# Cross-attention with low-rank weights: contexts computed for two groups at once, and Wo's low-rank part folded in earlier batches

## The reference

```python
def _lora_linear(x, W, A, B):
    return x @ W + SCALING * (x @ A @ B)          # R = 16, SCALING = 2
q = _lora_linear(hidden_states, Wq, Aq, Bq)       # 32 heads
k = _lora_linear(traces, Wk, Ak, Bk)              # 8 heads, each repeated for 4 query heads
v = _lora_linear(traces, Wv, Av, Bv)
scores = jnp.einsum('bhqd,bhtd->bhqt', q, k) / jnp.sqrt(HD)
attn = jax.nn.softmax(scores, axis=-1)
context = jnp.einsum('bhqt,bhtd->bhqd', attn, v)
out = _lora_linear(context, Wo, Ao, Bo)
return hidden_states + out
```

## Time and profile before

| | |
|---|---|
| timed executions | 675.72, 675.79, 678.38 us; median 675.79 |
| profiled execution | 678.06 us, its span 676.3 us |
| mean granted clock of PE | 0.947 |
| busy in the span | PE 98%, weight loads 78%, DVE 76%, ACT 69%, POOL 56% |
| contexts (L1532) | 1024 hardware matmuls, 70.3 us |
| DMA | 125.07 MB, 59.6% of 16 engines' time |

### The profile page before, as it was taken

The page is one execution under the profiler, slowest core; times in us unless marked ns, Lnnn a source line. Parts: engine busy times, 40 slices in busy tenths (PEclk is TensorE's granted clock), DMA queues, the critical chain, the costliest instruction groups (busy, mean ns, idle before and its releaser), DMA issues.

```text
span 676.3 us, 13385 instructions
## 1 busy us (share of the span) xinstructions
PE 662.5 (98%) x4220; PEld 528.2 (78%) x4220; DVE 512.7 (76%) x1161; ACT 467.6 (69%) x1462; POOL 375.9 (56%) x325
## 2 busy tenths in 40 slices
PE   9999999999999999999999999999899999999998
PEld 6798777877877887887887788787676788888886
DVE  4768887787788778778777877878887898855542
ACT  5558888888888888888888888887678443222220
POOL 3548785843762584386358438535867005776632
PEclk9999999999999999999999999999899999999999
DMA  8956655675665567556656646667676335655331
GB/s 268 355 171 211 207 182 164 196 212 167 174 197 183 158 195 227 162 179 195 198 149 201 210 157 183 197 187 211 186 225 205 107 120 172 202 187 186 126 121 66
DMA packets 103829, 125.07 MB, mean 185 GB/s; under 512 B 9280, under 2 KB 85312, under 8 KB 103760
## 3 DMA queue, kind: packets, MB, share of 16 engines
q1 hardware_dynamic: 103760, 124.23, 59.6%
HBM read 86.18 MB, written 38.01 MB: 184 GB/s over the span
## 4 chain that ended last, share of the span: by engine, by line
PE 82%; DVE 8%; ACT 4%; DMA 3%; issue 2%; SPq 1%; DVEq 0%
PE banks L1484 20%; PE banks L1677 17%; PE banks L1482 10%; PE banks L1502 9%; PE banks L1532 8%; PE banks L1519 8%; PE banks L1543 6%; DVE neg_max L1142 2%; ACT banks L930 2%; PE banks L1463 2%; DVE turned_sb L1163 2%; DMA raw<-xt 1%; PE banks L1450 1%; DVE max_parts L1151 1%; DMA raw<-ct 1%
## 5 line engine op out<-in xcount | busy, mean ns | idle before, releaser
L930 ACT ACTIVATE banks<-banks,neg_max 128x256 f32<-128x256 f32 x512 | 229.9, 452 | 29.8 <-DVE neg_max L1142 24.6
L812 POOL TENSOR_TENSOR q_stack<-turned_sb,head_mask 8x512 fp32r<-8x512 f32 x128 | 136.0, 1062 | 172.8 <-DVE turned_sb L1163 167.1
L1142 DVE TENSOR_REDUCE neg_max<-banks 128x2 f32<-128x512 f32 x256 | 175.0, 686 | 41.9 <-PE banks L1502 38.9
L941 ACT ACTIVATE probs_t<-banks 128x512 f32<-128x512 f32 x256 | 155.0, 605 | 48.4 <-PE banks L1519 48.0
L1484 PE MATMUL banks<-x_both,w_hi 128*128 128x512 f32 x448 | 162.9, 396 | 0.1
L1482 PE MATMUL banks<-x_both,w_lo 128*128 128x256 f32 x448 | 118.6, 280 | 0.0
L1502 PE MATMUL banks<-k_stack,q_stack 96*128 96x256 f32 x512 | 109.8, 296 | 0.7 <-DMA q_stack<-q_parts 0.7
L1502 PEld LDWEIGHTS banks<-k_stack,q_stack 96*128 96x128 f32 x512 | 81.3, 190 | 35.4 <-issue 25.8
L930 ACT ACTIVATION_READ_ACCUMULATOR banks<-banks,neg_max 128x1 f32 x512 | 106.7, 208 | 0.0
L1519 PE MATMUL banks<-q_stack,k_stack 104*128 104x512 f32 x256 | 102.4, 400 | 0.0
L1482 PEld LDWEIGHTS banks<-x_both,w_lo 128*128 128x128 f32 x448 | 84.5, 189 | 9.2
(11 more groups left out here) (156 smaller groups left out, 1154.7 us busy)
## 6 DMA issues: line engine op xcount, KB each, us to landing
q_stack<-q_parts SPq DMA_DIRECT2D x192, 128.0 KB, 3.0
q_parts<-q_stage SPq DMA_DIRECT2D x64, 256.0 KB, 3.5
raw<-ct SPq DMA_DIRECT2D x32, 256.0 KB, 3.5
raw<-xt SPq DMA_DIRECT2D x32, 256.0 KB, 3.8
scales<-r_rows SPq DMA_DIRECT2D x64, 128.0 KB
context<-ctx_stage SPq DMA_DIRECT2D x64, 128.0 KB, 3.7
stage<-xn SPq DMA_DIRECT2D x16, 512.0 KB, 5.4
w_hi<-context SPq DMA_DIRECT2D x14, 512.0 KB, 7.0
```

Source lines behind the costliest of these rows:

```text
L812: nc.gpsimd.tensor_tensor(q_stack[rows, u % RING, heads], turned_sb[rows, u % 2].unsqueeze(1).broadcast_to([M_ROWS, 2, S]), head_mask[rows ...
L930: last = nc.scalar.activation(score_bank(s)[:, S * h:S * (h + 1)], score_bank(s)[:, S * h:S * (h + 1)], ACT.Exp, bias=neg_max[:, u % 2, i: ...
L941: nc.scalar.activation(probs_t[:, u % 2, t, 2 * hp:2 * hp + 2, :].rearrange("p a b -> p (a b)"), st_bank[j % 2], ACT.Exp, scale=-1.0).then ...
L1142: nc.vector.tensor_reduce(out=neg_max[:, u % 2, 2 * c:2 * c + 2], in_=score_bank(s).rearrange("p (h t) -> p h t", h=2), axis=AXIS, op=ALU. ...
```

## The change

Contexts of the groups of batches 0 to 6 are computed for two groups at once (`context_pair`, with a third buffer for probabilities in `w_sum`): each strip has one of two groups and two of its four heads, 512 columns. DVE normalizes both at once (`normalize_pair`, in the slot with c = 3 of every second group), SP stores them by `store_pair`. Batch 7 keeps single contexts. Since heads lie in another order in the paired context, the rows of Wo and Ao are put in that order outside of the kernel.

Wo's fold moves to batches 1 to 4, one tile in each of the slots 9, 17, 25 and 33, through one buffer (`p1_copy`) and the context bank: SP fetches the raw tile (`fetch_raw`), PE folds (`wo_fold`), DVE sums (`wo_total`, one slot later), SP stores the sum in DRAM (`keep_sum`). In batch 7 SP loads the sums (`load_sum`), and DVE or ACT and POOL cut them.

```diff
+            def wo_fold(b, s, n):
+                if n == 0:
+                    lora_o_ready(pe)
+                pe.wait_ge(ctx_done, b * NG + s // 4 - 2)
+                kt, half = n % KT, n // KT
+                nc.tensor.matmul(ctx_bank, lora_o[0][:, P * kt:P * (kt + 1)], lora_o[1][:, 512 * half:512 * (half + 1)],
+                                 start=True, stop=True).then_inc(wo_folded, 1)
...
+            def context_pair(b, u):
+                need(pe, ctx_done, b * NG + u)
+                need(pe, wo_summed, min(WO_TILES, 4 * (b - 1) + u // 2 + 1))
+                pe.wait_ge(st_exp, b * SLOTS + (4 * u + 8))
+                if u == 0:
+                    pe.wait_ge(v_moved, b + 1)
+                for t in range(2):
+                    for k in range(4):
+                        g, j = u + k // 2, k % 2
+                        last = nc.tensor.matmul(
+                            ctx_bank[HD * k:HD * (k + 1), :].rearrange("p (h n) -> p h n", h=2),
+                            v_sb[:, t, HD * (g % NG):HD * (g % NG + 1)],
+                            p_buf(b * NG + g)[:, t, j::2, :], start=(t == 0), stop=(t == 1),
+                            tile_position=(0, HD * k))
+                last.then_inc(ctx_mm, 2)
...
-                if c == 0 and not (first and u < 2):
-                    context(b, u - 2)
+                if c == 0:
+                    if b * NG + u - 2 >= PAIRED:
+                        context(b, u - 2)
+                    elif u % 2 and b * NG + u - 3 >= 0:
+                        context_pair(b, u - 3)
...
+            def wo_total(n):
+                dve.wait_ge(wo_folded, n + 1)
+                dve.wait_ge(wo_raw_in, DMA * (n + 1))
                 nc.vector.scalar_tensor_tensor(
-                    out=w_piece(f, 0), in0=fold_bank(f), scalar=LORA_SCALE, in1=w_raw_of(f),
-                    op0=ALU.mult, op1=ALU.add).then_inc(w_hi_done, 1)
+                    out=p1_copy[:], in0=ctx_bank, scalar=LORA_SCALE, in1=p1_copy[:],
+                    op0=ALU.mult, op1=ALU.add).then_inc(wo_summed, 1)
+
+            def wo_high(n):
+                dve.wait_ge(proj_mm, (NB - 1) * PER + PRO)
+                dve.wait_ge(*wo_landed(n))
+                nc.vector.tensor_copy(wo_split(n, 0), w_raw_o[wo_home(n)]).then_inc(wo_hi_dve, 1)
...
+            def normalize_pair(b, u):
+                for i in range(2):
+                    dve.wait_ge(r_spread[i], b * (4 * DMA) + DMA * (u // 2 + 2))
+                    dve.wait_ge(ctx_stored[i], b * (4 * DMA) + DMA * (u // 2 + 1))
+                dve.wait_ge(ctx_mm, b * NG + (u + 2))
...
+            def fetch_raw(n):
+                if 0 <= n < WO_TILES:
+                    need(sp, wo_kept, DMA * n)
+                    kt, half = n % KT, n // KT
+                    sp.dma_start(p1_copy[:], wo[kt, :, 512 * half:512 * (half + 1)]).then_inc(wo_raw_in, DMA)
...
+            def load_sum(n):
+                wait(wo_kept, DMA * (n + 1))
+                if n % KT >= 4:
+                    wait(wo_lo, n - 3)
+                sp.dma_start(w_raw_o[wo_home(n)], wo_dram[n]).then_inc(wo_landed(n)[0], DMA)
```

More of the change, by code:

```diff
@@ L282, in fold_tile, with wo_home, wo_landed, wo_split @@
         def fold_tile(f):
-            base = FOLD_Q if f < FOLD_O else FOLD_O
-            return (f - base) % KT, (f - base) // KT
+            return (f - FOLD_Q) % KT, (f - FOLD_Q) // KT
         def w_raw_of(f):
-            return w_raw[f % W_RING] if f < FOLD_O else w_raw_o[f % 4 + 4 * (f >= FOLD_O + KT)]
+            return w_raw[f % W_RING]
+        def wo_home(n):
+            return n % 4 + 4 * (n >= KT)
+        def wo_landed(n):
+            return wo_in[wo_home(n)], DMA * (n % KT // 4 + 1)
+        def wo_split(n, part):
+            kt, half = n % KT, n // KT
+            return wo_piece(part, kt, half)
+        def fold_of(b, s):
+            k, off = divmod(s - FOLD_AT, FOLD_PACE)
+            if 1 <= b <= FOLD_BATCHES and s >= FOLD_AT and off == 0:
+                return 4 * (b - 1) + k
+            return None
         def lora_o_ready(engine):
@@ L644, in last_body @@
                 send(6)
+                wait(wo_lo, 6)
                 load_rows(0, 0)
@@ L1306, in slot @@
                 if last:
[L1307 to L1310 removed]
+                    for n in split_tiles(s):
+                        if n < KT:
+                            wo_high(n)
+                tile = fold_of(b, s - 1)
+                if tile is not None:
+                    wo_total(tile)
                 if c == 3 and here:
                     reciprocal(b, u)
[L1313 to L1314 removed]
+                if c == 3:
+                    if b * NG + u - 2 >= PAIRED:
+                        normalize(b, u - 2)
+                    elif u % 2 and b * NG + u - 3 >= 0:
+                        normalize_pair(b, u - 3)
                 if last:
```

240 lines of the change are left out of this document (142 added, 98 removed).

## The result

The changed kernel takes **804.48 us** (median of four: 801.54, 803.38, 805.57, 810.00) beside 677.0 us of the kernel before in the same comparison: a ratio of **1.190** with an interval of 1.187 to 1.193. It is 19% slower, where 2% faster was forecast. The profiled execution took 805.57 us, its span is 803.5.

The account below looks back on a forecast made before the run. PE was taken as the bound, full in the middle batches and held up in batch 7. Gains 9.0 + 10.9 = 19.9 less new stops 6.4 gave net 13.5: 675.8 - 13.5 = 662.3 us, range 655 to 669 (0.80).

Parts of the forecast that it names:

- the part on the fold: Moving Wo's fold to batches 1 to 4, with its SP and DVE work, was costed at 0, range 0 to 3 us.
- The pairs: Batches 0 to 6: one PE entry and exit saved per pair, 0.32 us each, 28 pairs, 9.0 us.
- the page's rule: Rival on PE's pairs: columns stream once whatever the type, 0.73 us saved a pair, 20.4 us, 651 us; chance 0.02.
- The fold: PE: 16 matmuls of 0.24 us, 3.8 us, leave batch 7 and enter batches 1 to 4; 0 in the sum.
- More than a slot to spare: Batches 1 to 4, context bank: pair normalized in DVE's slot 7, fold in 9; a slot is 1.8 us.
- The stop of 4.4 us ahead of slot 12: Batch 7: PE's context due at 478.8 gets its bank at about 483.2, as SP's queue waits for POOL's lows.
- After slot 12 ... I find nothing longer: Rest of batch 7: no longer stop; q6's restack is there about 495.6, PE asks at 495.
- 10.9: Batch 7's present losses, all to go without the fold: 8.3 us waits, 1.0 behind stops, 1.6 lower clock.
- the forecast 6.4: New losses in batch 7: stop 4.4 us, lower clock 1.6, casts delaying POOL 0.4.
- SP sets the pace of all of batch 7: Rival: each of four laps late by 3 to 4 us, 16.6 instead of 6.4, 672.5 us; chance 0.20.
- The slower rival: Batches 1 to 4: DVE waits for Wo's raw tile; 3.0 us late loses 21 us, 683 us; chance 0.04.
- nothing or little: Rival: the middle batches give back what the pairs gain, 672.4 to 679.2 us; chance 0.07.

Follow-up runs that it names:

- e1: Changed kernel with each pair spread (2 x 32 x 512) issued as two DMAs of 32 x 512: 704.13 us, ratio 1.041 to the kernel before.
- e10: e8 plus an extra DMA of 2 x 32 x 512 behind each pair spread, which nobody waits for: 749.50 us, ratio 1.107.
- e5: e1 with the second group's spreads issued ahead of the restack of q, as in e2: 685.76 us, ratio 1.015.
- e7: e1 with each store of a single context in batch 7 (2 x 64 x 256) made two DMAs of 64 x 256: 692.98 us, ratio 1.026.
- e2: Changed kernel with the second group's spreads issued ahead of the restack of q, shape unchanged: 759.29 us, ratio 1.123.
- e8: Changed kernel with three edits: pair spreads 32 x 512, second group's issued early, batch 7's single contexts stored as 64 x 256: 678.12 us, ratio 1.003.
- e4: Kernel before with each spread (4 x 32 x 256) made two DMAs of 2 x 32 x 256: 765.24 us, ratio 1.130.
- e9: e8 without the fold in batches 1 to 4, Wo's low-rank part left out of the output: 674.94 us, ratio 0.998.
- e13: e8 with the pair normalized in two halves in batches 0 to 6, the second one slot later: 703.16 us, ratio 1.039.
- e12: e8 with batch 7's loads of tiles 4 and 5 put behind q4's store, group 0's spread, pair -2's store, restack and row sums: 677.15 us, 1.000.
- e14: e12 with the same reordering done for q5 and q6 in batch 7: 680.28 us, ratio 1.004.
- e11: e8 plus an extra DMA of 32 x 2 x 512 behind each pair spread, same bytes as in e10: 693.66 us, ratio 1.023.

## Why the prediction was wrong, point by point

**The step that failed** is in the part on the fold: the spread of the second group "now stands behind the restack and the next row sums too", and "the restack (1.7), the two issues (0.9) and a landing of some 1.5 us leave it about 1 us", so I costed the whole move at 0 to 3 us. The place was seen rightly, the landing was not. No row gave the 1.5 us, and it fits neither shape: a spread lands 4.2 us behind its issue in the kernel before, 5.9 in the changed one (least 5.1) and 2.1 in e1. An estimate from that: with 5.9 in place of 1.5 the slack of 1 us becomes a wait of 3.4 a pair, where DVE waited 3.8. Even the old shape's 4.2 would have left a wait of 1.7. That the access pattern had changed from 4 x 32 x 256 to 2 x 32 x 512 was in the diff, and I did not cost it. Even with the right landing this step would have given only DVE's waits: e10 shows that the shape also makes all the others late, whether anyone waits for it or not.

**Its size.** Of 128 us, 100 go with the shape (e1), 18 with the place (e5) and 11 with the stores of batch 7 (e7), a second DMA with a slowest dimension of 2 in the same diff, which the sum did not name. With the place alone corrected 45 go (e2), so the two causes overlap in the changed kernel: a wait is only as long as the landing is longer than the slack.

**The pairs** (9.0 us forecast) came out right. PE in the changed kernel, which answers to the earlier trace rows:

```profile
370.94 0.28 PE L1608 MATMUL banks<-x_both,w_lo 128*128 128x256 f32 x1
371.15 1.92 PE L1675 MATMUL banks<-probs_t,v_sb 128*32 128x512 f32 x16
373.00 0.50 PE L1628 MATMUL banks<-k_stack,q_stack 96*128 96x256 f32 x2
373.34 0.40 PE L1645 MATMUL banks<-q_stack,k_stack 104*128 104x512 f32 x1
```

From 371.06 (0.12 behind the L1608) to 373.00 is 1.94, and 0.10 more until L1645: 2.04 us for a pair where 2.1 was forecast. In e8 two groups with a full PE and no fold take 14.27 instead of 14.68: 0.41 a pair instead of 0.32. But not all of it is the pairs': in e4, which has single contexts, two groups without a stop of PE take 14.60 (114.66 to 129.26), and against that a pair gains 0.33, 28 x 0.33 = 9.2 us. The rival *the page's rule* would have given 0.73.

**The fold** costs 0.24 us of PE a tile in the middle (14.51 against 14.27). The sum had 0, because the same 3.8 us leave batch 7; e8 and e9 show the first half (3.2 us). The second half is not shown: e8 is 1.5 us longer from the last pair on. "More than a slot to spare" was wrong: with the second half of the normalization one slot later, the fold stops PE 16 times (e13).

**Batch 7.** The stop of 4.4 us ahead of slot 12 is there in e8, between 481.85 and 486.27, forecast from 478.8 to 483.2, and its cause was SP's order (e12). But it comes with 6.8 us at the lower level where 3.2 were taken, and smaller stops of 1 to 2.5 us follow at 499, 509 and 524, so that e8 is at +1.5 us behind the last pair where -4.8 was forecast. "After slot 12 ... I find nothing longer" was true of each stop and wrong for their sum. What is new there comes to 12.8 us (10.9 + 0.3 of gain, and +1.5 came out), or 16.6 with the fold's columns that left, in place of the forecast 6.4. That is nearer to the rival *SP sets the pace of all of batch 7*; that e12 and e14 move the lateness from lap to lap speaks for it too.

**The slower rival** had the wrong mechanism: the raw tile of Wo. It needed a DMA chain to be late by some 3 us in front of DVE, at a price of 683 us. A DMA was late, by more, in front of the same engine, in all 28 pairs and not in 16, and it was the spread. The rival *nothing or little* is what e8 gives, not the changed kernel: its batches 0 to 6 together come out at +0.7 in place of -8.6 (-4.8 with the fold's columns), so the middle does give back what the pairs gain. The fold's columns (3.2 to 3.8 us) and the longer stretch once a batch (some 7 us) take it, which that rival did not name.

## What to carry to other kernels

When a diff changes the access pattern of a DMA, compare the slowest dimension of both sides with the old one before anything else, even for small transfers of constant size: with a slowest dimension of 2 the 128 KB landed 5.9 us behind their issue, with 4 it was 4.2, with 32 (two DMAs of half the bytes) 2.1; and in a place where no one waited for it the 2 cost 56 us more than the 32 (e10, e11). Put a large dimension outermost (32 here), if need be by two DMAs in place of one. Where the time from issue to landing of unrelated DMAs rises at once (here 3.5 to 5.4 us while the overall DMA share falls from 0.60 to 0.54), look for one transfer that sits on few engines, and not for too many bytes.

## What the runs showed of the hardware

- A DMA with a slowest dimension of 2 starts its 64 packets of 2 KB eight in 0.32 to 0.52 us and the last eight in 0.84 (changed kernel); the same bytes with 32 have all their packets started 0.96 us after the first (0.99 to 1.95), not 3.8 (1.29 to 5.12).
- An extra DMA of 128 KB behind each of 56 spreads, that nobody waits for, costs 0.28 us each with a slowest dimension of 32, 0.48 with 4 and 1.27 with 2. The Trainium skill (DMA: Bandwidth & Descriptors, Rules for kernel authors) says that an outermost dimension below 16 confines the DMA to that many engines; the runs agree: the extra DMA raises its semaphore 3 times with a 2, 5 times with a 4 and 16 times with a 32, and with a 2 two of the sixteen shares of the stores of q are late (e10). They add what it costs the others.
- The profiled execution of the kernel before has a mean granted clock of 0.947, and 0.95 from 340 to 442 us; later executions of the same kernel have 0.995 to 1.000 and take the same time (675.5 to 680.4 us). In e8 the same stretch has 1.00:

```profile
340.00:442.00 102.00, 100.69 (x618) 78.49 (x618) 82.14 (x210) 86.59 (x296) 59.74 (x54) 1.00 0.63 192
```

  A matmul of 512 columns comes 0.233 us after the last in the one and 0.235 in the other, and two groups of single contexts take 14.68 us at 0.95 and 14.60 in e4 at 1.00. So the 0.95 of this record is some 0.5% of the time at most, not 5%. Only the stretches at 0.5 count: there the same distance is 0.43 (changed kernel).
